# Another opening for a paged-attention kernel: keys and values projected first, splits of weights and inputs set at other places of the first steps

## What is computed

```
q = _rope(_rmsnorm(x @ Wq.T, q_norm_w), pos)
k = _rope(_rmsnorm(x @ Wk.T, k_norm_w), pos)
v = x @ Wv.T
scores = einsum('bqhd,bkhd->bhqk', q, concat(kc, k)) * SCALE     # kc, vc: gathered pages of the cache
scores = where(valid, scores, -1e30)
o = einsum('bhqk,bkhd->bqhd', softmax(scores), concat(vc, v))
x = x + o @ Wo.T
x = x + x @ W.T + SCALING * lora_out                             # gates: top 2 of logits + LANG_BIAS * one_hot(language)
```

## Time and profile before

| | us |
|---|---|
| median of 3 timed runs | 1185.21 (1185.18 to 1185.74) |
| profiled execution | 1183.14 |
| its span, first to last instruction | 1181.3 |
| TensorE busy | 1146.3 (97%) |
| ScalarE busy | 932.1 (79%) |
| VectorE busy | 923.3 (78%) |
| GpSimd busy | 766.3 (65%) |
| TensorE waits for GpSimd's rotated queries, once | 9.1 |
| TensorE waits for the first low part of the weights, once | 8.3 |

### The profile page before, as it was taken

One profiled execution on the slowest core, in us unless ns is written; L12 is line 12 of the kernel. 1 busy time (PEld: TensorE's weight loads), 2 busy tenths in 40 slices (PEclk: granted clock), 3 DMA queues, 4 the chain that ended last, 5 costly groups with the idle time before them and its releaser, 6 DMA issues.

```text
span 1181.3 us, 20774 instructions
## 1 busy us (share of the span) xinstructions
PE 1146.3 (97%) x6912; PEld 1024.1 (87%) x6912; DVE 923.3 (78%) x1880; ACT 932.1 (79%) x1830; POOL 766.3 (65%) x838
## 2 busy tenths in 40 slices
PE   4799999999999999999999999999999999999898
PEld 3688898998899898989988998989899889989787
DVE  6788888787778777887877787778878777877746
ACT  3787888888888888888888888888888888888741
POOL 5566666677676667676766766677667667666500
PEclk9899999999999999999999999999999999999999
DMA  6423412221232222122212222221232122111001
GB/s 240 127 79 97 148 53 89 95 88 54 94 95 70 72 94 95 51 91 94 88 55 95 94 66 77 94 95 50 93 94 83 58 93 92 59 67 55 19 1 72
DMA packets 53626, 98.11 MB, mean 83 GB/s; under 512 B 8592, under 2 KB 25872, under 8 KB 53264
## 3 DMA queue, kind: packets, MB, share of 16 engines
q1 hardware_dynamic: 41232, 63.21, 15.4%
q0 software_dynamic: 12288, 33.57, 9.6%
HBM read 90.45 MB, written 6.29 MB: 82 GB/s over the span
## 4 chain that ended last, share of the span: by engine, by line
PE 87%; DVE 5%; ACT 3%; issue 2%; DMA 1%; SPq 1%; POOL 0%; DVEq 0%; POOLq 0%
PE ps_s L1011 18%; PE ps_w L282 17%; PE ps_w L280 17%; PE ps_w L281 17%; PE ps_w L1042 9%; PE ps_w L1133 3%; PE ps_w L1115 2%; PE ps_s L993 2%; PE ps_w L1019 2%; ACT ps L527 2%; DVE pt_lo L664 1%; ACT ps L533 1%; DMA y<-wo 1%; DVE ps L727 1%; PE ps_w L1032 1%
## 5 line engine op out<-in xcount | busy, mean ns | idle before, releaser
L406 POOL DMA_INDIRECT kv_raw<-kv,rows x256 | 253.6, 991 | 93.8 <-issue 62.7
L527 ACT ACTIVATE ps<-ps,negmax 128x640 f32<-128x640 f32 x256 | 211.9, 828 | 97.9 <-DVE negmax L727 97.8
L664 DVE TENSOR_TENSOR pt_lo<-ps_w,pt_hi 128x512 fp32r<-128x512 f32 x322 | 209.9, 683 | 75.7 <-ACT pt_hi L538 74.4
L533 ACT ACTIVATE ps<-ps,recip 128x640 f32<-128x640 f32 x256 | 213.0, 832 | 67.4 <-DVE recip L734 67.4
L727 DVE CUSTOM_DVE_ANT_0 ps<-ps_s,mask 128x640 f32<-128x640 f32 x256 | 203.8, 814 | 1.1 <-PE ps_s L1011 1.1
L280 PE MATMUL ps_w<-w_hi,xt_hi 128*128 128x512 f32 (+1 forms) x512 | 188.9, 369 | 10.0 <-DVE w_lo L664 8.3
L282 PE MATMUL ps_w<-w_hi,xt_lo 128*128 128x512 f32 (+1 forms) x512 | 173.6, 339 | 0.0
L281 PE MATMUL ps_w<-w_lo,xt_hi 128*128 128x512 f32 (+1 forms) x512 | 173.1, 338 | 0.0
L427 POOL TENSOR_TENSOR rot<-u,cos 128x640 f32<-128x640 f32 x64 | 101.5, 1587 | 110.0 <-DVE u L783 110.0
L538 ACT ACTIVATE pt_hi<-ps_w 128x512 fp32r<-128x512 f32 x256 | 151.7, 593 | 17.8 <-PE ps_w L1042 15.0
L1042 PE MATMUL ps_w<-cst,ps 128*128 128x128 f32 x1024 | 154.1, 273 | 6.6 <-DVE pt_lo L664 5.9
(11 more groups left out here) (155 smaller groups left out, 2625.0 us busy)
## 6 DMA issues: line engine op xcount, KB each, us to landing
xt_hi<-xsplit SPq DMA_DIRECT2D x56, 256.0 KB, 3.2
xt_lo<-xsplit SPq DMA_DIRECT2D x56, 256.0 KB, 3.7
w_raw<-wqkv SPq DMA_DIRECT2D x56, 192.0 KB, 3.9
wo_raw<-wo SPq DMA_DIRECT2D x56, 128.0 KB, 4.2
kv_raw<-kv,rows POOLq DMA_INDIRECT x256, 3.9
xsplit<-xt_hi SPq DMA_DIRECT2D x8, 256.0 KB, 2.9
xsplit<-xt_lo SPq DMA_DIRECT2D x8, 256.0 KB, 4.2
y<-x SPq DMA_DIRECT2D x2, 1024.0 KB, 7.4
```

The costliest lines, as they stand in the source:

```text
L406: pool.indirect_dma_start(kv_raw[:, g % 2, t, :], None, kv[:, :], bass.IndirectOffsetOnAxis(rows[:, g % B, t:t + 1], 0)).then_inc(s_kv[g % ...
L527: nc.scalar.activation(ps[:, h, :], ps[:, h, :], ACT.Exp, bias=negmax[:, s % 2, h:h + 1], scale=-1.0, accum_out=rowsum[:, s % 2, h:h + 1]) ...
L533: nc.scalar.activation(ps[:, h, :], ps[:, h, :], ACT.Copy, scale=recip[:, s % 2, h:h + 1]).then_inc(a_norm, 1)
L664: return nc.vector.tensor_tensor(out_ap, full, hi.bitcast(F32), ALU.subtract)
```

## The change

The own opening runs ahead of the loop on every engine, and the loop begins at step 0 instead of -2.

- SyncE loads the first key/value weights in two halves ahead of the query weights, the norm weights ahead of the second half of the first x blocks, and the key numbers (for the masks) into the wo buffer behind them. The natural x comes in single blocks.
- GpSimd issues the first gather behind the landing of the second query block, then computes the root for group 0, then issues the second gather. It takes no other part in the rotation of group 0.
- ScalarE and VectorE split in the new order. X blocks 2 and 3 are split into the second weight buffer, not in use then. The two pi reduction has two parts, not three.
- VectorE multiplies group 0 by the plain norm weights at once, makes both rotation products and the sums, and the root is multiplied in at the end, by head: two on ScalarE, three on VectorE.
- TensorE projects keys and values of group 0, queries of 0 and of 1, turns the cached keys, projects keys and values of 1, and turns the rest. Keys and values of group 2 are projected in the middle of step 0.
- The first two masks are written ahead of step 0, the other six in steps 1 and 2 (two at the front, one near the end). The biases are written at the end of step 8.
- The first wo splits all lie in step 0. `W_AT` and `WO_AT` are one step later, head 1 is spread up to step 8, and `W_MID` and `WO_MID` put one piece into the middle of a step. `split_x` of blocks 4 to 7 moves from the end of a step to its middle.

```diff
-TWO_PI_A = 6.28125
-TWO_PI_B = float(np.float32(int((TWO_PI - TWO_PI_A) * 2**20) / 2**20))
-TWO_PI_C = float(np.float32(TWO_PI - TWO_PI_A - TWO_PI_B))
+TWO_PI_A = round(TWO_PI * 2**12) / 2**12
+TWO_PI_B = float(np.float32(TWO_PI - TWO_PI_A))
...
-        W_AT.setdefault((0, 0, 1, 2, 2, 3, 4, 4)[j] if h == 1 else B * h - 11 + j, []).append((h - 1) * B + j)
-WO_AT = {s: [s] for s in range((HK - 1) * B + 2)}
+W_AT = {2: [2], 3: [4], 4: [6], 5: [7]}
+W_MID = {1: 0, 2: 1, 3: 3, 4: 5}
...
+    W_AT[n - 2] = [n]
...
+WO_MID = {6: 3, 7: 5}
...
+    WO_AT[n + 1] = [n]
```

SyncE and GpSimd:

```diff
-            for g in range(2):
-                gather_dma(g)
-            pool.wait_ge(s_tables, 32)
+            pool.wait_ge(s_w0[1], 16)
+            gather_dma(0)
             pool.wait_ge(p_init, 2)
-            for s in range(-2, G + 1):
+            inverse_norms(0)
+            gather_dma(1)
+            pool.wait_ge(s_nw, 16)
+            for s in range(G + 1):
```

VectorE, in the opening and in `step(s)`:

```diff
+            dve.wait_ge(a_sincos, 1)
+            nc.vector.tensor_scalar(sin[:, :, HALF:D], sin[:, :, 0:HALF], -1.0, None, ALU.mult).then_inc(d_tab, 1)
+            wait(dve, a_kv, 0)
+            wait(dve, a_q, 0)
+            dve.wait_ge(s_nw, 16)
+            nc.vector.tensor_tensor(u[:].rearrange("p h d -> p (h d)"), raw[:, 0, 0:QW + D], nw[:].rearrange("p h d -> p (h d)"),
+                                    ALU.mult).then_inc(d_u, 1)
+            sums_of_squares(0)
+            dve.wait_ge(d_tab, 1)
+            times_sine(0)
...
+            wait(dve, p_rstd, 0)
+            for h in range(2, NH):
+                nc.vector.tensor_scalar(rot[:, h, :], rot[:, h, :], rstd[:, h:h + 1], None, ALU.mult).then_inc(d_scaled, 1)
+            cached_keys(0)
+            split_x(2)
+            turned_queries(0)
+            new_keys(0)
+            dve.wait_ge(s_kpos, 16)
+            masks(0, 2)
...
+                if s in (1, 2):
+                    masks(3 * s - 1, 3 * s + 1)
...
+                if HB <= s + 3 < B:
+                    split_x(s + 3)
+                if s == 0:
+                    first_wo_split(0)
+                    first_wo_split(1)
...
+                if s == B:
+                    biases()
```

TensorE:

```diff
-            for s in range(-2, G + 1):
-                if s == -1:
-                    pe.wait_ge(s_cst, 16)
+            pe.wait_ge(d_xlo, 1)
+            project_keys_values(0)
+            project_queries(0)
+            project_queries(1)
+            pe.wait_ge(s_cst, 16)
+            turn_cached_keys(0)
+            project_keys_values(1)
+            turn_queries(0)
+            turn_new_keys(0)
+            for s in range(G + 1):
                 step(s)
```

466 lines of the change are left out of this document (276 added, 190 removed).

## The result

The changed kernel takes 1175.14 us (median of 4 runs, 1174.34 to 1177.25), the kernel before, run beside it, 1185.20 (4 runs, 1185.18 to 1185.74): a ratio of 0.9917, 95% interval 0.9900 to 0.9934. The forecast was 1173.4 in a range of 1171.0 to 1177.5. The profiled execution took 1174.34, its span 1172.5.

The account below looks back on a forecast made before the run. TensorE's matmuls bound the steady steps, so gains lay in the opening's waits and steps 1 to 9. The terms 11.7 - 1.1 + 2.9 - 0.2 - 1.5 = 11.8 took the median of 1185.2 to 1173.4, range 1171.0 to 1177.5.

Parts of the forecast that it names:

- opening, to the first maximum: New prologue: first score maximum at 24.3 instead of 36.03, a gain of 11.7 us, range +0.7 to -3.
- step 0: First loop step: more VectorE work, an x split and four wo splits, loses 1.1 us, bounds 0 and 2.
- steps 1 to 9 without the biases: Early steps: excess delay falls from 4.75 to 1.9, gain 2.9 us (bounds 1.5 and 4.4), less 0.2.
- biases: End of step 8: eight bias instructions moved out of the prologue lose 1.5 us, bounds 1.2 and 1.76.
- behind step 10: Steady steps: shifting later pieces by one step costs 0, at worst 0.2 for each of seven heads.
- the 0.2 for steps 6 and 7: Steps 6 and 7: an extra wo piece ahead of the new keys' low part loses 0.2 us.
- Rival 2: Step 0: TensorE's clock falls, some 4 us of work take 2 us longer, total 1175.5; chance 0.10.
- Rival 1: Opening: the prologue runs later than summed, price 2.5 us, total 1176; chance 0.18.
- Rival 3: Steps 1 to 9: the pauses hold everything, excess 0.4 instead of 1.9, total 1171.9; chance 0.15.
- Rival 4: Steady steps: GpSimd's product starts ahead of the wo piece, every step pays 0.86, total 1221; chance 0.02.
- Rival 5: Opening: the wait for the first scores is only moved, nothing gained, total 1185; chance 0.03.

Follow-up runs that it names:

- e1: The changed kernel with VectorE's middle piece (w or wo) split behind the new keys' kt_lo, no longer ahead of it: 1171.98 us.
- e3: The changed kernel with 18 idle transposes of the identity matrix added on TensorE in step 0: 1173.96 us.
- e5: The changed kernel with 28 idle transposes on TensorE ahead of its first projection: 1174.66 us.
- e10: The changed kernel with the eight biases two by two in steps 9 to 12, between sums of squares and second reciprocal: 1172.65 us.
- e11: The changed kernel with the edits of e1, e10 and e3, and the second group's keys and values projected ahead of the cached keys' transposes: 1169.64 us.
- e13: e11 with the x splits of groups 4 to 7 at the end of steps 1 to 4, not the middle: 1172.07 us.
- e2: The changed kernel with one bias in each of steps 9 to 16, ahead of o_lo, instead of all eight ending step 8: 1177.71 us.
- e9: The changed kernel with the first group's gathers issued at once, not waiting for the second piece of the query weights: 1175.45 us.

## Why the prediction was right, and where not

**By its parts**, in us of the profiled executions (a gain is positive):

| | predicted | measured |
|---|---|---|
| opening, to the first maximum | +11.7 (+8.7 to +12.4) | +11.1 |
| step 0 | -1.1 (-2 to 0) | -0.7 |
| steps 1 to 9 without the biases | +2.9 - 0.2 | +0.2 |
| biases | -1.5 (-1.76 to -1.2) | -1.15 |
| behind step 10 | 0 | -0.65 |
| sum | 11.8 | 8.8 |

**The opening** was right nearly link by link: first matmul 8.15 for 8.15, second queries 16.27 for 15.8, cached keys' transposes 19.22 for 19.3, first scores 23.62 for 23.4, first maximum 24.89 for 24.3. The term's range was needed: the six equal openings give gains of 9.9 to 11.6. Its reading that the queries' end sets the next link holds only by a hair: in the changed kernel the queries end at 15.49 and ScalarE is through with the sines at 15.53, while in e1, e3, e5 and e10 TensorE had ended earlier and waited 1.01 to 1.40 us, not 0.78, for ScalarE.

**Step 0** lost 0.7 where 1.1 was put down, but by other items. The x split was held by GpSimd's product, as said (1.74 us instead of 0.69); that product ends at 30.58, and `u`, which needs it, starts 0.47 later, for +0.5 in the sum. Timelines of GpSimd and VectorE:

```profile
29.32 1.26 POOL L458 TENSOR_TENSOR wr<-nw,rstd 128x640 f32<-128x640 f32 x1
...
29.39 1.74 DVE L742 TENSOR_TENSOR w_lo<-y,w_hi 128x512 fp32r<-128x512 f32 x1
31.05 0.81 DVE L878 TENSOR_TENSOR u<-raw,wr 128x640 f32<-128x640 f32 x1
31.79 0.15 DVE L839 RECIPROCAL recip<-rowsum 128x1 f32<-128x1 f32 x1
31.90 0.82 DVE L805 TENSOR_TENSOR m<-u,sin 128x640 f32<-128x640 f32 x1
```

What came back is in the last line: the product with the sines took 0.82 and not the 1.9 to 2.0 of a steady step, as it started 0.04 us ahead of GpSimd's rotation (31.94), which took 2.22 instead of 1.57. With the clock held the step takes 17.28 (e3; 17.28 and 17.30 in e11 and e13), 0.16 above that of before, so 0.56 of the loss is the clock, a term that the sum did not have, and the wo splits cost next to nothing in length; their price is that TensorE starves beside them.

**Steps 1 to 9** is the term that was mis-sized: 0.2 for 2.7. Without the 0.2 for steps 6 and 7 its lower bound was 1.5. Two steps of the working failed. "The weight piece in the middle (0.46) falls into the 0.6 pause behind the keys": the pause is behind the *last* kt_lo, and the piece was put ahead of it; the order of instructions said so, and I took the length of the pause from the row but not its side. e1 prices it at 2.0 us with step 7. The other is the clock, 0.87 in step 1. With both undone, and the biases in a better place, the excess of steps 1 to 9 is 1.44 us (e11: 155.39 against nine steps of 17.105), and 1.9 was predicted. The x splits, forecast 0.4 late in steps 1 to 4, took 0.68 to 0.85 us, 0.0 to 0.17 more than alone.

**The biases** cost 1.15 us (step 8 at 18.50, and at 17.35 and 17.34 without them in e10 and e2), just under the lower bound of 1.2. The reason was right: all eight together take 1.15 us there (184.20 to the next maximum at 185.35), and all of it is lost. The size was off because the 1.76 of the earlier trace rows were read as eight plain ones; the first of these took 824 ns and the others 217 or 218, while GpSimd's sums ran until 31.03. A better place avoids the whole loss (e10).

**Rival 2**, given 0.10, came true: its price of 2 us is 1.4 in this profile, and it belongs at the start of step 1 rather than in step 0. My argument against it was that before the fall of the earlier trace rows there had been an idle stretch of 9.07 us. But the trace of before already shows that so much was not needed. TensorE's idle stretch begins at 22.08, and the busy table of before reads (columns as above):

```profile
24.00:25.00 1.00, 0.00 (x0) 0.00 (x0) 0.62 (x2) 0.00 (x0) 1.00 (x1) 0.78 0.00 0
```

The clock fell in the third microsecond of the stretch; the earlier trace rows show only that it was still low after its end. In step 0 of the changed kernel short pauses with little work between them did it too, and so in each of the ten profiles without idle work. The Trainium skill ("TensorE: Matmul & The Clock Gate", What's actually happening) has the throttled state as the default that activity releases; the rows agree, and e3 and e11 are that rule put to use. **Rival 1** (opening late, 2.5 us) did not come in the profiled run, but its cause is real: in e3, e5, e9 and e13 the opening was 0.8 to 2.8 us later, for a landing each time. **Rival 3** (all pauses hold) falls with steps 2 to 4 at 17.75 to 17.86. **Rival 4** did not come, the steady step is 17.107; e2 shows that it was a real edge, at 0.43 us a step. **Rival 5** falls.

**Why the median was nearer than the sum.** The profiled execution of after should have been 1171.3 and was 1174.34, 3.0 above. The forecast was moved up by the 2.1 us between profile and median of before; for after that distance is 0.8. So 1.3 us of the error of the sum is hidden in the final number, by luck. Some 0.65 us are lost behind step 10, 0.56 of them after the last sum on VectorE, in the output's transfers. The change need not cost them: from the first maximum of step 10 to the end e11 takes 969.47 us, the kernel before 969.45, the changed one 970.10.

## What to carry to other kernels

Before an instruction is moved "into a pause", read which instruction ends that pause, and put it behind the one that others wait for: the same 0.47 us cost little on one side of kt_lo and all of it on the other. Ask of a pause what the neighbour engine does in it, since eight tiny VectorE instructions cost 0 in one and 0.43 us each in another. And where work is piled on one engine so that TensorE gets short pieces, count the clock as part of the price, and fill the pauses with idle work if nothing else can.

## What the runs showed of the hardware that was not expected

- **A VectorE instruction of eight elements waits as long as one of 512** behind a GpSimd product of 128x640: 1.23 us (e2) against 0.22 (e10), with one SBUF tile and one column as inputs. The Trainium skill ("GPSIMD Engine Reference", Key points) names contention for instructions with two SBUF inputs or in a 2-port mode; it fits the rows, and these show a stop until the product's end rather than a slowdown.
- **Who starts first wins.** When VectorE's product began 0.04 us ahead of GpSimd's, it ran its plain 0.82 us and GpSimd's was stretched from 1.57 to 2.22. The kernel before has the same pair in its opening: 0.82 from 26.68 on the earlier trace rows, and 2.17 for GpSimd's product from 26.73 on.
- **The granted clock in the records does not show the slow start.** In the changed kernel, from 11.2 to 13.9 us, the passes of 512 columns start 0.42 to 0.54 us apart and later 0.23, while PEclk reads 1.00; after 5 us of idle transposes (e5) they start, where they do not wait for weights, 0.23 to 0.33 apart from the first one on. The first passes of a program are to be judged by their pitch.
- **The clock fell after pauses of at most 1.6 us** in the changed kernel, with TensorE busy 2.07 of the 5 us from 35 to 40, and 18 idle transposes in those pauses kept it at 1.00 (e3).
